# Fetching whole blocks of rows by GpSimd in two sorted-edge aggregations of a graph network

## What is computed

```python
def _sage_conv(x, src, dst, Wl, Wr, b):
    agg = jax.ops.segment_sum(x[src], dst, num_segments=N)
    cnt = jax.ops.segment_sum(jnp.ones((src.shape[0],), x.dtype), dst, num_segments=N)
    return agg / jnp.maximum(cnt, 1.0)[:, None] @ Wl.T + b + x @ Wr.T
# layer 1: x = x + conv2(relu(conv1(h)))
# layer 2: x = x + segment_mean(relu([h[src], h[dst], edge_attr] @ W1 + b1) @ W2 + b2, src)
```

## Time and profile before

| | |
|---|---|
| median of 3 runs | 4394.75 us |
| lowest, highest | 4372.95, 4398.56 us |
| span of the profiled execution | 4375.3 us |
| its own time, as far as recorded | the span; no other figure is recorded for it |
| PE busy, DVE busy | 3697.5 us (85%), 3679.1 us (84%) |
| ACT busy, POOL busy | 2589.0 us (59%), 3032.7 us (69%) |
| products on PE | 64,703 |
| mean granted TensorE clock | 0.949 |

### The profile page before, as it was taken

How to read it: one execution, slowest core, us unless ns; L and a number is a source line. 1 busy time by engine, 2 the same in 40 slices (tenths; PEclk the granted TensorE clock), 3 DMA queues, 4 the chain that set the end, 5 groups by cost and what they waited for, 6 DMA issues and landing times. The chain is left out here.

```text
span 4375.3 us, 174335 instructions
## 1 busy us (share of the span) xinstructions
PE 3697.5 (85%) x64703; PEld 3536.1 (81%) x64703; DVE 3679.1 (84%) x6413; ACT 2589.0 (59%) x5168; POOL 3032.7 (69%) x2760
## 2 busy tenths in 40 slices
PE   3699999999977999999758888888888888888876
PEld 3688888888877999999747887877788887788876
DVE  7799999999988888888758888887878878888876
ACT  3455555555545666666537666666666666666664
POOL 1688888888854666666517777777777777777771
PEclk9899999999999999999868999999999999999998
DMA  5233333333326545555335555555555555555552
GB/s 104 68 84 83 83 82 83 83 83 85 82 64 170 118 118 118 118 118 119 68 110 162 163 169 175 174 159 159 164 166 174 174 162 161 160 165 174 174 153 65
DMA packets 481209, 557.42 MB, mean 127 GB/s; under 512 B 180610, under 2 KB 437873, under 8 KB 480870
## 3 DMA queue, kind: packets, MB, share of 16 engines
q1 hardware_dynamic: 395782, 451.91, 36.7%
q0 software_dynamic: 84032, 103.47, 10.2%
q10 hardware_dynamic: 1266, 0.31, 0.0%
HBM read 478.48 MB, written 76.90 MB: 127 GB/s over the span
## 5 line engine op out<-in xcount | busy, mean ns | idle before, releaser
L1388 POOL DMA_INDIRECT sorted_edges<-edge_rows,edge_index x1566 | 1535.3, 980 | 568.0 <-issue 559.1
L969 POOL DMA_INDIRECT conv_got<-parts_table,conv_index x1060 | 1324.5, 1250 | 467.2 <-issue 235.7
L1079 ACT CAST conv_rows<-conv_rows_ps 128x384 bf16<-128x384 f32 x2226 | 1020.3, 458 | 671.4 <-PE conv_rows_ps L993 654.8
L993 PE MATMUL conv_rows_ps<-parts,conv_hot_t 128*128 128x192 bf16 x8268 | 1049.8, 246 | 72.4 <-DVE conv_hot_t L1145 72.4
L1010 PE MATMUL conv_sums<-conv_rows,conv_hot_d 128*128 128x193 bf16 (+1 forms) x8268 | 1052.6, 247 | 3.0 <-DMA conv_got<-parts_table,conv_index 3.0
L993 PEld LDWEIGHTS conv_rows_ps<-parts,conv_hot_t 128*128 128x128 bf16 x8268 | 696.4, 97 | 94.7 <-issue 55.4
L1450 PE MATMUL edge_sums<-edge_parts,edge_hot 128*128 128x64 bf16 (+1 forms) x15582 | 597.2, 200 | 201.0 <-DVE acc L1640 196.7
L1450 PEld LDWEIGHTS edge_sums<-edge_parts,edge_hot 128*128 128x128 bf16 x15582 | 556.8, 102 | 220.9 <-DVE acc L1640 165.0
L1010 PEld LDWEIGHTS conv_sums<-conv_rows,conv_hot_d 128*128 128x128 bf16 x8268 | 720.4, 98 | 4.2 <-DMA conv_got<-parts_table,conv_index 3.7
L1435 PE MATMUL edge_a_ps<-parts,edge_hot_t 128*128 128x64 bf16 x15582 | 548.7, 197 | 36.4 <-issue 25.3
L1145 DVE TENSOR_SCALAR conv_hot_t<-conv_slot_row,node_of 128x768 bf16<-128x768 bf16 (+1 forms) x1484 | 542.1, 407 | 22.0 <-PE conv_rows_ps L993 14.6
(11 more groups left out here) (193 smaller groups left out, 4717.5 us busy)
## 6 DMA issues: line engine op xcount, KB each, us to landing
edge_slot_row<-slot_rows SPq DMA_DIRECT2D x371, 224.0 KB
edge_edges<-sorted_edges SPq DMA_DIRECT2D x371, 224.0 KB
conv_slot_row<-slot_rows SPq DMA_DIRECT2D x424, 192.0 KB
conv_slot_row<-slot_rows SPq DMA_DIRECT2D x318, 160.0 KB
edge_dst_row<-dst_rows SPq DMA_DIRECT2D x261, 192.0 KB
edge_attr<-in_edge_attr SPq DMA_DIRECT2D x260, 192.0 KB
sorted_edges<-edge_rows,edge_index POOLq DMA_INDIRECT x1566
conv_got<-parts_table,conv_index POOLq DMA_INDIRECT x1060
```

Of the source, the lines that this page charges most:

```text
L969: pool.indirect_dma_start(got[g][:, f, 0:PARTS * D], None, k.parts_table, bass.IndirectOffsetOnAxis(ap=index[h][:, g, at:at + 1], axis=0)) ...
L993: mm = pe.matmul(rows_ps[(bs * h + i) % banks][:, at:at + PARTS * D], hot_t[home[g]][:, v, u * P:(u + 1) * P], k.parts[:, 2 * (GU * g + u) ...
L1079: act.copy(rows[i % bufs][:, 0:n, 0:PARTS * D], rows_ps[(bs * h + i) % banks][:, 0:n * PARTS * D].rearrange("p (u d) -> p u d", u=n)).then ...
L1388: pool.indirect_dma_start(k.sorted, bass.IndirectOffsetOnAxis(ap=index[h][0:used, at:at + 1], axis=0), rows[j][0:used, t, :], None).then_i ...
```

## The change

Blocks now have two kinds, by `WHOLE` = "PPF" in both aggregations: blocks 2, 5, ..., 50 (17 of 53) are F, the other 36 are P.
- **P blocks** expand all 49 units by products; POOL fetches nothing for them. A group now has four steps (2, 2, 2 and 1 unit), `bs` is 28 and `cut` 10. Slot rows and `hot_t` have 896 columns in place of 768 or 640.
- **F blocks** have no `hot_t`, no `expand`, no copies and no slot-row loads. POOL fetches the source row of every edge in edge order, 30 indirect DMAs of 128 rows, into five `got` buffers (WG = 5, up to 7 tiles each). PE adds them with 2 x 30 products (`reduce_whole`), and `hot_d` is made for 30 tiles in five groups. The destination of each edge is taken only if it found a slot (`picked`, `choose_dst`); where both kinds agree, the second `plane` and half of `scatter`'s columns are left out for an F block.
- All indices are made at the start of `conv` by DVE, and POOL's fetches are a straight list without a loop. A `got` buffer is fetched again once the F block before has been added from it.
- In `conv1` the new buffers lie in `k.x` (65 of 98 windows), and SP loads those windows again from the input at the end. In `conv2` they have memory of their own.
- `hot_d` buffers go round in threes over a whole PPF cycle (`home_d`; the last group of the F block takes the buffer of two groups earlier); `conv2` now has three buffers each, not four, but four `rows` and PSUM banks, not three.
- The hardware loop's body is six blocks (`ROUND`), not two.

```diff
+WHOLE = {"conv1": "PPF", "conv2": "PPF"}
+ROUND = 6
...
-        fetched = [1 + g % 2 for g in range(NG)]
-        steps = [[(u, min(u + 2, GU - n)) for u in range(0, GU - n, 2)] for n in fetched]
+        steps = [(u, min(u + 2, GU)) for u in range(0, GU, 2)]
...
-        bs, cut, banks, bufs, most = NG * ns, 8, 2 if sorting else 3, 3, (GU - min(fetched)) * P
+        bs, cut, banks, bufs = NG * ns, 10, 2 if sorting else 4, 4
...
-        home = (0, 1, 2, 0, 1, 2, 1) if sorting else (0, 1, 2, 3, 0, 1, 2)
+        home = (0, 1, 2, 0, 1, 2, 1)
...
+        home_d = [x % 3 for x in range(starts[-1])]
+        if starts[-1] % 3 == 1:
+            home_d[-1] = 1
...
+        room = k.x[:].rearrange("p w d -> p (w d)").bitcast(BF16)[:, 0:of_x] if sorting else o.tmp("room", [P, of_x], BF16)[:]
...
 def load(t):
                 if sorting:
                     s.store_row(sp, t.b)
+                    if t.kind == "P":
+                        sp.wait_ge(s.row_stored, 16 * (t.b + 1))
+                if t.kind == "F":
+                    return
...
+            if sorting:
+                sp.wait_ge(s.row_stored, 16 * NB)
+                sp.wait_ge(reduced, Turn(kinds, whole[-1]).made + WG)
+                sp.dma_start(k.x[:, 0:x_taken, :], k.x_rows[:, 0:x_taken, :]).then_inc(x_back, 16)
+                sp.wait_ge(x_back, 16)
...
+            pool.wait_ge(begun, 2)
+            pool.wait_ge(index_made, 1)
+            for f, b in enumerate(whole):
+                for g in range(WG):
+                    if f >= 1:
+                        pool.wait_ge(reduced, Turn(kinds, whole[f - 1]).made + g + 1)
+                    for t in tiles_of(g):
+                        pool.indirect_dma_start(got[g][:, t - GU * g, 0:PARTS * D], None, k.parts_table, bass.IndirectOffsetOnAxis(ap=index[:, f, t:t + 1], axis=0)).then_inc(got_landed[g], 16)
...
+            def reduce_whole(t, g):
+                pe.wait_ge(hot_d_made, t.made + g + 1)
+                pe.wait_ge(got_landed[g], 16 * len(tiles_of(g)) * (t.f + 1))
+                if g == 0:
+                    sums_free(t)
+                for x in tiles_of(g):
+                    mm = add_up(t, g, x - GU * g, got[g][:, x - GU * g, 0:wide_cols])
+                mm.then_inc(reduced, 1)
...
+                    if i in (3, 8) and t.kind == "F":
+                        reduce_whole(t, i // 5)
+                    hooks(i, last, t, t1, t2)
...
+                for j in range(3):
+                    if t.n >= 0 and t.kind == "F":
+                        reduce_whole(t, 2 + j)
+                    if j < 2 and sorts(t2) and (t.n < 0 or t.kind == "F"):
+                        s.prefix(pe, t2.b, t2.n, 1 + j)
...
+            dve.tensor_scalar(index, node, 1.0, float(ROWS - 1), ALU.subtract, ALU.min).then_inc(index_made, 1)
```

More of the change, by code:

```diff
@@ L906, in in_turn, with at @@
-            for b in range(2 * pairs, NB):
-                second(b, b % 2, MANY)
-                if b + 1 < NB:
-                    first(b + 1, (b + 1) % 2, MANY)
-        def sorts(b, lag):
-            return sorting and (not isinstance(b, int) or 0 <= b + lag < NB)
+            def at(c, i=None):
+                return [Turn(kinds, c + d, i) for d in (-1, 0, 1, 2, 3)]
+            for c in range(-ahead, 1):
+                first(*at(c))
+                if c < 0:
+                    second(*at(c))
@@ new lines, in in_turn, with here @@
+            second(*at(0))
+            first(*at(1))
+            second(*at(1))
+            first(*at(2))
+            with eng.Fori(0, rounds) as i:
+                for r in range(ROUND):
+                    second(*at(2 + r, i))
+                    first(*at(3 + r, i))
+            for c in range(2 + ROUND * rounds, NB):
+                second(*at(c))
+                if c + 1 < NB:
+                    first(*at(c + 1))
+        def here(t):
+            return not t.known or 0 <= t.b < NB
@@ L929, in _ @@
+            load(Turn(kinds, 0))
             if not sorting:
@@ L1068, in _, with hooks @@
-            move(NB - 1, MANY)
+            def hooks(i, last, t, t1, t2):
+                if i in (1, 2, 4) and sorts(t1):
+                    s.scatter(pe, t1.b, t1.n, i // 2, t1.sums)
+                if i == 5 and sorts(t2):
+                    s.count(pe, t2.b, t2.n)
+                if i == 6 and sorts(t2):
+                    s.prefix(pe, t2.b, t2.n, 0)
+                if i == 7 and sorts(t1):
+                    s.turn(pe, t1.b, t1.n)
+                if i == 7 and t.n >= 1:
+                    move(last)
@@ new lines, in first @@
+            def first(last, t, t1, t2, t3):
+                if t.n < 0:
+                    for j in range(PIECES):
+                        if sorts(t1):
+                            s.scatter(pe, t1.b, t1.n, j, t1.sums)
+                    s.count(pe, t2.b, t2.n)
+                    s.prefix(pe, t2.b, t2.n, 0)
+                    if sorts(t1):
+                        s.turn(pe, t1.b, t1.n)
+                    return
+                for i in range(cut):
+                    if t.kind == "P":
+                        expand(t, i)
+                    if i < 2 and t.n >= 1 and last.kind == "P":
+                        rest_of(last, bs - 2 + i)
+                    if i >= 2 and t.kind == "P":
+                        reduce(t, i - 2)
+                    if i in (3, 8) and t.kind == "F":
+                        reduce_whole(t, i // 5)
+                    hooks(i, last, t, t1, t2)
@@ L1159, in take @@
+            def take(t):
+                dve.wait_ge(reduced, t.made + t.groups)
+                dve.tensor_scalar(moved_to[:], k.iota[:], k.shift_to[:, bass.ds(t.b, 1)], None, ALU.is_equal)
+                both = sums[t.h][:, 0:2 * wide_cols].rearrange("p (v d) -> p v d", v=2)
                 if sorting:
```

466 lines of the change are left out of this document (222 added, 244 removed).

## The result

The changed kernel takes 4358.5 us (median of 8 runs, 4332.8 to 4366.7) beside 4394.8 us for the kernel before (8 runs, 4368.4 to 4400.7): ratio 0.994, 95% interval 0.992 to 0.996. The forecast was 4260, with a range of 4215 to 4305, so the result lies outside it.

The account below looks back on a forecast made before the run. It took PE and DVE, both nearly full, to bound conv1 and PE alone conv2. Gains of 53 us in conv1 and 82 in conv2, together 135, took the median from 4394.75 to 4260 us, range 4215 to 4305.

Parts of the forecast that it names:

- Product, work of P and F: PE in both aggregations: 0.083 us a product, P blocks 1.66 us more, F blocks 9.6 less, 6.3 off per three blocks.
- `conv2`, F turn: F block in conv2: 5.4 us of work plus waits of 0.75 and 0.3, 6.5; three blocks 39.8 against 45.0.
- the walk: Step-by-step timing of the F turns through the engines, looking for waits; three blocks 60.9 us in conv1, 39.8 in conv2.
- `conv1`, F turn: F block in conv1: sorting chain makes PE wait about 3.5 us for hot_t; turn 14.9 us, three blocks 59.7 before clock.
- The clock: PE's clock falls to half in each F turn of conv1, 1.2 us net, giving 60.9 us per three blocks.
- So today's loops run without new fetches: PE's loops in both aggregations: the queue's 82 transfers were taken to show that two-block bodies need no new instruction fetches.
- the rival: PE's six-block loop fetched anew each round in both stages: 45 us, 40 partly hidden, total 4300; chance 0.11.
- The forecast's own sign against itself: Instruction queue over the whole span: the forecast is wrong if it moves some hundred transfers.
- Fetching: POOL's 30 transfers per three blocks stay hidden: 38.3 us in conv2, nearer 55 in conv1; POOL some 75% busy in conv2.
- a rival of that kind (0.05): Fetching becomes the bound: transfers of 2.06 us in conv2, three blocks 62 us, total 4635; chance 0.05.
- Ends: Stage ends: 2.3 us a stage for fills and indices, 3.3 for the last two P blocks, 1 for x in conv1.
- Sum: Both aggregations with ends: conv1 gains 53 us and conv2 82, together 135, giving 4260.

Follow-up runs that it names:

- e3: Changed kernel with DVE's masks for the first group of the block after an F block made earlier in the F turn; 4325.0 us.
- e8: Changed kernel with the F turn's work on PE and DVE ordered anew, nothing added or left out; 4300.8 us.
- e4: Changed kernel with 44 idle products on PE behind each F block's last products in conv1; 4306.5 us.
- e2: Changed kernel with PE's instructions of both aggregations written out straight, without a hardware loop; 4293.9 us.
- e6: Changed kernel with POOL fetching for the first F block of each aggregation alone, on another chip; 5829 us, ratio 0.939 to the kernel before there.
- e9: Changed kernel with straight PE code, 44 idle products in conv1's F turns and early masks in conv2 alone; 4260.2 us.
- e11: Kernel before with loop bodies of four blocks instead of two; 4440.7 us.
- e10: Changed kernel with the order of e8 in both stages, straight PE code and 24 idle products in conv1's F turns; 4247.2 us.
- r1_after: Changed kernel itself, run once more and on another chip; 6667 us, ratio 1.076 to the kernel before there.

## Why the prediction was wrong, point by point

- *Product, work of P and F.* Right in kind, a little low. A clean cycle of `conv2` holds 39.7 us of busy PE where the forecast had 38.7:

```profile
1495.74:1537.35 41.61, 39.67 (x465) 38.59 (x465) 32.63 (x58) 25.61 (x60) 25.93 (x28) 1.00 0.47 110
```

- *`conv2`, F turn.* The waits were 1.9 us (0.64, 0.67, 0.24, 0.38) where the walk had 1.05. It missed those for `block_sum` in the P turn and for the copy. With the 1.0 us of work above, the clean cycle is 41.6 against 39.8: 31 us over 17 cycles. This is the first step that failed, since the walk put at nothing every wait that it did not find. `e3` shows that 1.1 us a cycle was order alone.
- *`conv1`, F turn.* The mechanism and the gap were right, the sum over three blocks was not: the clean cycle is 62.8 against 60.9, another 32 us. The P turns hold DVE waits that the walk had not (1.23 us for a `hot_d` buffer and 1.48 for a `hot_t` buffer, both held by PE), and PE waits twice 0.6 us for `slot_hot` behind them. `e8` won 1.0 us of the 1.9 back by order.
- *The clock.* Right that it falls in each F turn of `conv1` and not in `conv2`'s clean cycles. Its price in a clean cycle, 1.2 us forecast, is 0.9 (`e4`). Where an issue gap joins, it costs more; with it the clock took 22 to 27 us of the stage.
- *"So today's loops run without new fetches ... Against it: a stage now branches back 8 times where it did 25".* This is the second step that failed: the loop was held at a chance of 0.11 and its cost left out of the sum, and it is the case. Its size was right: 45 us forecast for the rival, 36 to 42 measured (`e2`). The forecast's own sign against itself (some hundred instruction transfers) came with 262. The count of branches was a bad argument. What counts is whether the body is kept: 24 rounds of two blocks cost nothing, and of 8 rounds of six each of the 7 branches back costs a stall. It also brings the clock down in `conv2`, which the rival left out.
- *Fetching.* Right on the chips where the kernel before takes 4371 to 4395 us (hidden by the comparison with `e6`, 1.25 us a transfer); POOL is busy 64% of `conv2`, not 75%. On the other chip the change is 7.6% slower than the kernel before. The forecast had a rival of that kind (0.05), but by slow transfers and not by signals that come late.
- *Ends.* Between the last `move` of `conv1` and the first of `conv2` 92.8 us became 93.9, where 2.3 for the fills and indices and 1 for `x` were forecast. The `x` load delays nothing.
- *Sum.* By the stages' clocks `conv1` gained -2 to 3.5 us and `conv2` 25, where 56 and 85 were forecast from `move` to `move` (53 and 82 with the ends). The rest of the gain is in a stage that was not changed. From its first to its last `edge_sums` product the edge stage takes 2004.6 us before and 1988.6 in the changed kernel:

```profile
L1450 PE MATMUL edge_sums<-edge_parts,edge_hot x15582: 190/193/247, 2324.3 to 4328.9; 128*128 128x65 bf16 x200
```

```profile
L1526 PE MATMUL edge_sums<-edge_parts,edge_hot x15582: 190/193/247, 2303.0 to 4291.6; 128*128 128x65 bf16 x200
```

It takes 1998 to 2005 us in all three profiles with the old aggregations and 1982 to 1989 in all nine with the new ones (the other chip left out). No run asks why, so this stays open. It means that the two stages that were changed gave only 24 to 29 us. That `e9` measures 4260, the number forecast, is partly chance: its stages gained 42 and 74 us, not 56 and 85, and the edge stage, which the forecast left alone, gave it 18.

It was therefore two cases at once: the forecast's walk, short by 1.8 us a cycle in each stage (63 us in all, the larger part), and the third rival on top (36 to 42 us). The range of 3 us per three blocks in `conv1` was wide enough for the walk's error, the one of 1 us in `conv2` was not.

## What to carry to other kernels

Before a loop body grows, count its instructions on the fullest engine, weight loads and waits included: on PE a body of 1570 was kept here and one of 2070 was not, and past that every branch back cost 2 to 6 us, whatever the body was made longer for. It shows as idle time "issue" once a round and in the instruction queue's transfers. When products are taken out of a block, what they hid comes out: fill the holes by reordering, and keep the clock with idle products where a hole stays, but look up when an input lands before a consumer is moved forward. A change that leans on long runs of small indirect transfers can turn round on a chip where the other engines stand while they run, so measure it on more than one. And before a cycle's length is called the price of a transfer, look at when its packets moved.

## What the runs showed of the hardware that was not expected

- A stall of the loop costs more than its gap: 37.2 us of gaps at 11 branches back, but 62 us of stage (`e11`).
- Straight code needed 229 instruction transfers, nearly as many as the stalling loop's 262, and cost no gap in the aggregations.
- The clock can fall after the work has begun again: in `e10` products behind a 1.7 us gap run at full speed at first and at half some 2 us later, in about every second cycle.
- 44 idle products took 0.9 us off a clean cycle and 1 to 3 off one with an issue gap (`e4`).
- On one chip the updates of semaphores came a median of 21 us late while POOL issued its fetches (`r1_after`), though the transfers themselves kept their pace of 1.25 us; in the changed kernel's other two profiles the median is 0.01 us.
- The last projection runs at a granted clock of 0.92 in some executions of the same code and at 0.52 in others, 47 and 73 us long.
